# Row maxima of attention scores: turned from columns to rows by VectorE's block transposes instead of TensorE and ScalarE

## The reference

```
x = x + (softmax(Q K^T / 4) V) Wo^T + bo     # Q from layernorm(x), K and V from the context,
                                             # 16 heads of 16 features
h = layernorm(x)
w = softmax(h G) cut to its two largest of 8 experts
out = x + sum_e w_e * down_e(silu(gate_e h) * (up_e h)) + sum_e w_e * loraB_e(loraA_e h)
```

## Time and profile before

| what | value |
|---|---|
| median of 3 runs | 115.64 us (114.97 to 116.44) |
| profiled execution, its own time | 115.25 us |
| its span, first to last instruction | 113.5 us |
| granted TensorE clock, mean | 1.000 of full speed |
| busy TensorE, VectorE | 104.7 us (92%), 89.8 us (79%) |
| busy ScalarE, GpSimd | 70.8 us (62%), 61.5 us (54%) |

### The profile page before, as it was taken

How to read it: one execution, slowest core, us unless ns; L and a number is a source line. 1 busy time by engine, 2 the same in 40 slices (tenths; PEclk the granted TensorE clock), 3 DMA queues, 4 the chain that set the end, 5 groups by cost and what they waited for, 6 DMA issues and landing times.

```text
span 113.5 us, 2548 instructions
## 1 busy us (share of the span) xinstructions
PE 104.7 (92%) x868; PEld 79.6 (70%) x868; DVE 89.8 (79%) x185; ACT 70.8 (62%) x127; POOL 61.5 (54%) x91
## 2 busy tenths in 40 slices
PE   4976999997999999999999999979998899999990
PEld 4656868775776766758676696858565889888680
DVE  5454199998989899799999996968599765589941
ACT  0414562389899869878888899897963504335110
POOL 2268910499859803990588746482729981442000
PEclk9999999999999999999999999999999999999999
DMA  2994788762498003910000400000000000110034
GB/s 60 283 365 190 258 306 249 271 213 78 69 396 326 12 6 129 378 58 0 3 0 6 141 0 6 1 1 0 6 0 0 0 0 0 49 52 3 0 133 147
DMA packets 9405, 11.91 MB, mean 105 GB/s; under 512 B 1008, under 2 KB 6448, under 8 KB 9392
## 3 DMA queue, kind: packets, MB, share of 16 engines
q1 hardware_dynamic: 8672, 11.22, 28.3%
q10 hardware_dynamic: 720, 0.53, 1.5%
HBM read 4.34 MB, written 1.05 MB: 47 GB/s over the span
## 4 chain that ended last, share of the span: by engine, by line
PE 66%; DVE 10%; DMA 7%; POOL 5%; issue 5%; ACT 3%; SPq 1%; POOLq 0%; DVEq 0%
PE unit L766 18%; PE unit L872 12%; PE unit L840 9%; PE unit L773 8%; PE unit L859 7%; DMA wa<-wattn 4%; DMA qstack<-q_lo 3%; POOL attnT L491 3%; PE unit L913 2%; PE unit L911 2%; PE unit L912 2%; DVE rowmax L695 2%; POOL attnT_lo L492 2%; PE unit L846 1%; PE unit L799 1%
## 5 line engine op out<-in xcount | busy, mean ns | idle before, releaser
L695 DVE TENSOR_REDUCE rowmax<-unit 128x4 f32<-128x1024 f32 x32 | 37.5, 1212 | 1.7 <-PE unit L840 1.5
L604 ACT ACTIVATE probs<-unit 128x1024 f32<-128x1024 f32 x32 | 32.2, 1030 | 4.7 <-PE unit L859 4.4
L872 PE MATMUL unit<-probs,vaug 128*32 128x256 f32 x256 | 15.9, 383 | 0.0
L840 PE MATMUL unit<-kstack,qstack 63*128 63x256 f32 x128 | 14.1, 311 | 0.8 <-DVE rowmax L695 0.4
L840 PEld LDWEIGHTS unit<-kstack,qstack 63*128 63x128 f32 x128 | 9.6, 185 | 5.9 <-issue 3.0
L859 PE MATMUL unit<-qstack,kstack 64*128 64x256 f32 x128 | 13.3, 300 | 0.2
L491 POOL TENSOR_SCALAR attnT<-attnT,bias_sb 128x256 f32<-128x256 f32 x8 | 7.7, 957 | 8.6 <-ACT attnT_hi L541 8.2
L859 PEld LDWEIGHTS unit<-qstack,kstack 64*128 64x128 f32 x128 | 9.6, 185 | 3.6 <-issue 1.5
L627 ACT COPY hlT<-unit 128x384 f32<-128x384 f32 x8 | 3.7, 479 | 12.7 <-PE unit L906 12.7
L872 PEld LDWEIGHTS unit<-probs,vaug 128*32 128x32 f32 x256 | 7.3, 109 | 5.1
L459 POOL TENSOR_SCALAR vare<-mv 128x2 f32<-128x2 f32 x8 | 1.8, 223 | 13.2 <-DVE mv L645 12.9
(11 more groups left out here) (97 smaller groups left out, 227.1 us busy)
## 6 DMA issues: line engine op xcount, KB each, us to landing
kstack<-k_hi SPq DMA_DIRECT2D x8, 256.0 KB, 2.7
qstack<-q_hi SPq DMA_DIRECT2D x6, 256.0 KB, 2.8
xs<-x SPq DMA_DIRECT2D x4, 256.0 KB, 3.4
kstack<-k_lo SPq DMA_DIRECT2D x4, 256.0 KB, 2.7
out<-xs SPq DMA_DIRECT2D x8, 128.0 KB, 1.8
cT<-ctxT SPq DMA_DIRECT2D x3, 256.0 KB, 3.7
qstack<-q_lo SPq DMA_DIRECT2D x3, 256.0 KB, 2.9
wf<-wffn SPq DMA_DIRECT2D x1, 648.0 KB, 4.3
```

The source lines that it names most:

```text
L604: act.activation(probs[:, n % NPAIR], unit[PAIR[name, n] // 2][:], ACT.Exp, scale=SCALE).then_inc(exp_done, 1)
L695: dve.tensor_reduce(rowmax[:, b % 2, :, i // 4, :, i % 4].rearrange("p t j -> p j t"), unit[PAIR[name, n] // 2][:], AX.X, ALU.max)\
L840: ins = pe.matmul(dst[:, j, t], qs[rows, PLACE[i], t * P:(t + 1) * P], ks[rows, PLACE[i]], start=True, stop=True)
L872: ins = pe.matmul(dst[QUAD * j:QUAD * (j + 1), i], vaug[:, of % 3, t, 4 * g + j], probs[:, n % NPAIR, j % 2, t], start=(t == 0), stop=(t = ...
```

## The change

The maxima of a half are no longer transposed by TensorE and copied by ScalarE. VectorE does both: four block transposes, one for each 32 partitions of `rowmax`, write `mT` in SBUF. Each reads 32 partitions x 64 elements (two 32x32 blocks, for the two groups of 128 tokens) and writes 32 partitions x 64 elements that always start at partition 0. For that `rowmax` gets 32 columns for each half and group of tokens, of which 8 hold maxima and 24 are zeroed once by GpSimd, and `mT` gets 32 rows, of which the DMA still reads the first 8.

The eight `mrow` stages leave the lists of TensorE and ScalarE and come into VectorE's, each directly behind the fourth or eighth `max` of its batch. All other stages keep their order, but for `ones` (GpSimd's memsets), which goes from behind `minus:2` to the front of its list. PSUM banks that held an `mrow` result go to the next stage of the list without it.

```diff
 "vector":
-    ... max:0.0-3 ln1:2 q:1 max:0.4-7 max:1.0 ln1:3 max:1.1-7
-    u:0 max:2.0-3 u:1 max:2.4-7 u:2 max:3.0 o:0 max:3.1-2 ln2:0 max:3.3 u:3 max:3.4-5 u:4 max:3.6 o:1
-    ln2:1 max:3.7 u:5 route1:0 ...
+    ... max:0.0-3 mrow:0.0 ln1:2 q:1 max:0.4-7 mrow:0.1 max:1.0
+    ln1:3 max:1.1-3 mrow:1.0 max:1.4-7 mrow:1.1 u:0 max:2.0-3 mrow:2.0 u:1 max:2.4-7 mrow:2.1 u:2 max:3.0
+    o:0 max:3.1-2 ln2:0 max:3.3 mrow:3.0 u:3 max:3.4-5 u:4 max:3.6 o:1 ln2:1 max:3.7 mrow:3.1 u:5 ...
 "gpsimd":
-    ln1:0 zero:0 ln1:1 minus:1 zero:1 consts ln1:2 wolo minus:2 ones zero:2 ln1:3 ...
+    ones ln1:0 zero:0 ln1:1 minus:1 zero:1 consts ln1:2 wolo minus:2 zero:2 ln1:3 ...
 "tensor", "scalar":
-    mrow:0.0 mrow:0.1 mrow:1.0 ... mrow:3.1      (each at its place in the list)
...
-        rowmax = sb("rowmax", [P, 2, ST, 2, 2, PAIRS // 2])
-        mT = sb("mT", [PAIRS, 2, S], F32R)
+        rowmax = sb("rowmax", [P, 2, 2, ST, QUAD], F32R)
+        mT = sb("mT", [QUAD, 2, ST, P], F32R)
...
             if name == "mstack":
-                wait_freed(engine, "mrow", 2 * b + i)
+                engine.wait_ge(max_rows, 2 * b + i + 1)
                 engine.dma_start(qstack[b % NSTACK][ROWS:P:HALF]...[:, :, i],
-                                 mT[:, i].bitcast(F32)).then_inc(m_stacked[b % NSTACK][i], 16)
+                                 mT[0:PAIRS, i].bitcast(F32).rearrange("c t p -> c (t p)")).then_inc(...)
...
                 if name == "ones":
+                    pool.memset(rowmax[:, :, :, :, PAIRS:QUAD].bitcast(F32), 0.0).then_inc(row_pads, 1)
+                    pool.wait_ge(row_pads, 1)
...
-                if name == "mrow":                                        # ScalarE
-                    bank, turn = WORK[name, 2 * b + i]
-                    wait_made(act, name, 2 * b + i)
-                    if b:
-                        act.wait_ge(m_stacked[(b - 1) % NSTACK][i], 16 * ((b - 1) // NSTACK + 1))
-                    act.copy(mT[:, i], work[bank][0:PAIRS, 0]).then_inc(work_free[bank], 1)
...
+                if name == "mrow":                                        # VectorE
+                    if b:
+                        dve.wait_ge(m_stacked[(b - 1) % NSTACK][i], 16 * ((b - 1) // NSTACK + 1))
+                    dve.wait_ge(max_done, PAIRS * b + 4 * i + 4)
+                    dve.wait_ge(row_pads, 1)
+                    for n in range(P // QUAD):
+                        tokens = slice(n * QUAD, (n + 1) * QUAD)
+                        ins = dve.transpose(mT[:, i, :, tokens].bitcast(F32), rowmax[tokens, b % 2, i].bitcast(F32))
+                    ins.then_inc(max_rows, 1)
...
-                if name == "mrow":                                        # TensorE
-                    pe.wait_ge(max_done, PAIRS * b + 4 * i + 4)
-                    for t in range(ST):
-                        ins = pe.transpose(dst[0:PAIRS, 0, t * P:(t + 1) * P],
-                                           rowmax[:, b % 2, t, i].rearrange("p j c -> p (j c)"), ident[:])
-                    ins.then_inc(work_ready[bank], 1)
```

More of the change, by code:

```diff
@@ L43 @@
         k:0@0 xT:0@1 qh:0@1 qh:1@0 k:1@2 v:0@1 max:0.0@4 max:0.1@6 xT:1@2 max:0.2@0 max:0.3@4 q:1@2 v:1@3
[L44 to L56, removed]
+        max:0.4@4 max:0.5@6 max:0.6@0 k:2@2 max:0.7@4 attn:0.0@6 xT:2@3 attn:0.1@0 max:1.0@6 attn:0.2@4
+        attn:0.3@0 max:1.1@6 max:1.2@4 q:2@3 max:1.3@0 max:1.4@6 attn:0.4@4 k:3@2 max:1.5@0 xT:3@3 max:1.6@4
@@ new lines @@
+        attn:0.5@6 max:1.7@0 u:0.0@3 u:0.1@3 attn:0.6@4 max:2.0@0 attn:0.7@6 q:3@3 max:2.1@4 attn:1.0@6
+        max:2.2@0 u:1.0@2 max:2.3@4 attn:1.1@6 u:1.1@2 attn:1.2@0 attn:1.3@4 max:2.4@6 v:2@3 max:2.5@0
+        attn:1.4@4 max:2.6@6 u:2.0@2 max:2.7@0 attn:1.5@4 u:2.1@2 attn:1.6@6 attn:1.7@4 max:3.0@0 o:0@2
+        max:3.1@6 attn:2.0@4 u:3.0@3 max:3.2@0 attn:2.1@4 u:3.1@3 max:3.3@6 attn:2.2@0 attn:2.3@4 v:3@2
+        attn:2.4@6 max:3.4@4 max:3.5@2 u:4.0@1 u:4.1@1 attn:2.5@4 attn:2.6@6 max:3.6@2 x2T:0@0 o:1@1 low:0@0
@@ L57 @@
+        attn:2.7@2 max:3.7@4 attn:3.0@6 u:5.0@0 u:5.1@0 attn:3.1@2 attn:3.2@4 attn:3.3@6 glu0:0@0 x2T:1@1
+        glu1:0@2 o:2@3 attn:3.4@0 attn:3.5@4 low:1@2 attn:3.6@6 attn:3.7@0 u:6.0@3 u:6.1@3 u:7.0@2 u:7.1@2
+        x2T:2@3 glu0:1@0 hl:0@1 glu1:1@2 hl:1@3 low:2@4 o:3@0 down:0@1 glu1:2@0 hl:2@2 down:1@3 x2T:3@2
+        down:2@4 glu0:2@5 hl:3@2 low:3@4 glu1:3@1 glu0:3@2 hl:4@0 down:3@4 hl:5@0 down:4@5 hl:6@0 down:5@2
+        hl:7@0 down:6@1 down:7@0
     """,
     "scalar": """
-        biases c:0 cb k:0 xT:0 qh:0 qhih:0 qh:1 k:1 norm1:1 v:0 xT:1 q:1 mrow:0.0 wohi norm1:2 v:1 attn:0.0
@@ L60 @@
[L60 to L64, removed]
@@ L66 @@
+        x2T:1 glu1:0 attn:3.3-6 low:1 attn:3.7 norm2:2 ahi:6 x2T:2 exps:1 glu0:1 ahi:7 hl:1 hl:0 glu1:1 low:2
+        hl:2 exps:2 x2T:3 hl:3 glu0:2 glu1:2 low:3 exps:3 hl:4 glu0:3 glu1:3 hl:5 hl:6 hl:7
     """,
     "vector": """
-        minus:0 ln1:0 norm1:0 ln1:1 k:0 qh:0 k:1 qh:1 max:0.0-3 ln1:2 q:1 max:0.4-7 max:1.0 ln1:3 max:1.1-7
-        u:0 max:2.0-3 u:1 max:2.4-7 u:2 max:3.0 o:0 max:3.1-2 ln2:0 max:3.3 u:3 max:3.4-5 u:4 max:3.6 o:1
-        ln2:1 max:3.7 u:5 route1:0 route2:0 glu0:0 glu1:0 o:2 ln2:2 route3:0 route1:1 u:6 u:7 route2:1 glu0:1
@@ L71 @@
-        route3:1 glu1:1 o:3 ln2:3 route1:2 norm2:3 route2:2 down:2 route3:2 down:0 glu0:2 glu1:2 route1:3
-        route2:3 route3:3 glu0:3 weigh:6 glu1:3 weigh:7 down:4 down:3 down:5 down:6 down:1 down:7
+        minus:0 ln1:0 norm1:0 ln1:1 k:0 qh:0 k:1 qh:1 max:0.0-3 mrow:0.0 ln1:2 q:1 max:0.4-7 mrow:0.1 max:1.0
+        ln1:3 max:1.1-3 mrow:1.0 max:1.4-7 mrow:1.1 u:0 max:2.0-3 mrow:2.0 u:1 max:2.4-7 mrow:2.1 u:2 max:3.0
+        o:0 max:3.1-2 ln2:0 max:3.3 mrow:3.0 u:3 max:3.4-5 u:4 max:3.6 o:1 ln2:1 max:3.7 mrow:3.1 u:5
@@ L73 @@
+        route1:0 route2:0 glu0:0 glu1:0 o:2 ln2:2 route3:0 route1:1 u:6 u:7 route2:1 glu0:1 route3:1 glu1:1
+        o:3 ln2:3 route1:2 norm2:3 route2:2 down:2 route3:2 down:0 glu0:2 glu1:2 route1:3 route2:3 route3:3
+        glu0:3 weigh:6 glu1:3 weigh:7 down:4 down:3 down:5 down:6 down:1 down:7
     """,
     "gpsimd": """
-        ln1:0 zero:0 ln1:1 minus:1 zero:1 consts ln1:2 wolo minus:2 ones zero:2 ln1:3 k:2 q:2 xo:0 xo:1 k:3
+        ones ln1:0 zero:0 ln1:1 minus:1 zero:1 consts ln1:2 wolo minus:2 zero:2 ln1:3 k:2 q:2 xo:0 xo:1 k:3
@@ L202, in xattn_moe_kernel @@
         qzero = [sem(f"qzero{i}") for i in range(NSTACK)]
-        vones = sem("vones")
+        vones, row_pads = sem("vones"), sem("row_pads")
         wf_hi_ready, wf_parts = sem("wf_hi_ready"), sem("wf_parts")
@@ L694, in _ @@
                     dve.wait_ge(s_ready, n + 1)
-                    dve.tensor_reduce(rowmax[:, b % 2, :, i // 4, :, i % 4].rearrange("p t j -> p j t"), unit[PAIR[name, n] // 2][:],
+                    of_pair = rowmax[:, b % 2, i // 4, :, 0:PAIRS].rearrange("p t (j c) -> p j t c", c=4)[:, :, :, i % 4]
+                    dve.tensor_reduce(of_pair, unit[PAIR[name, n] // 2][:],
                                       AX.X, ALU.max)\
                         .then_inc(max_done, 1)
+                if name == "mrow":
[7 more added lines that the diff above has]
+                    ins.then_inc(max_rows, 1)
                 if name == "u":
@@ L779, in _ @@
             for name, b, i, at in plan("tensor"):
-                me = (name, 2 * b + i if name == "mrow" else b)
-                if me in WORK:
-                    bank, turn = WORK[me]
+                if (name, b) in WORK:
+                    bank, turn = WORK[name, b]
                     dst = work[bank]
                     if not (name == "u" and i):
-                        wait_banks(pe, me)
+                        wait_banks(pe, (name, b))
                 if name in ("xT", "x2T"):
```

10 lines of the change are left out of this document (6 added, 4 removed).

## The result

The changed kernel takes 122.56 us (median of 4 runs, 121.4 to 123.57) where the kernel before takes 115.31 us in the same comparison: the ratio is 1.0567, with a 95% interval of 1.0509 to 1.0625. By it the kernel is slower by 6.5 us; 5.5 us had been forecast.

A forecast was written before the change was run, and what follows sets the result against it. VectorE was taken as the bound once its reserve was used: eight stages of 1.03 us less 2.72 us of waits give 5.5 us, and 115.25 + 5.5 = 120.75, forecast as 120.7 us; range 117.7 to 122.4 us.

The forecast's parts named there:

- The bound: While the maxima are made, 15.3 to 69.6 us, VectorE is busy 51.60 of 54.30 us and has almost no room.
- 2.72 us of waits: VectorE's whole reserve up to `u:5`: four waits of 1.82 us together and a fifth of 0.90 us before `u:5`.
- The price of a transpose: One 32x64 transpose on VectorE: 0.25 us, extrapolated from 704 ns for 512 elements a partition and 445 ns for 256.
- full duration without overlap: The four transposes of an `mrow` stage run one after the other on VectorE: 4 x 0.25 = 1.00 us.
- L645's pairs: Two VectorE instructions without a wait take 0.25 us where 2 x 0.166 = 0.33, so the second costs 0.08 us less.
- The overlap case: Rival: a stage's transposes overlap on VectorE, 0.79 us a stage, 3.6 us slower, 118.9 us; chance 0.27.
- The stage: One `mrow` stage on VectorE, lost overlap and gap included: 0.09 + 0.03 + 1.00 - 0.09 = 1.03 us.
- the forecast put at nothing: VectorE's new waits for the pads and the last batch's `mstack` are for things long past and cost nothing.
- 8c - 2.72: Eight stages of 1.03 us on VectorE less its reserve of 2.72 us: `u:5` comes 5.5 us later.
- its saved time becomes waiting: TensorE falls behind from a delay of 0.94 us on; its 0.25 us saved at each `mrow` become waiting.
- The rival that TensorE stays the bound: VectorE's waits up to `u:5` swallow stages of at most 0.34 us; not slower, 113.6 us; chance 0.07.
- the six chain pieces: Six pieces of TensorE's L846 on the chain of waits, 0.22 to 0.32 us each, 1.6 us in all.

The follow-up runs named there:

- The addition alone: Kernel before with all its TensorE and ScalarE work, plus four block transposes of a spare tile on VectorE at each place of the change: ratio 1.0584.
- four spare matmuls: Changed kernel plus four unneeded matmuls in TensorE's list, one ahead of `attn:0.3` and three ahead of `max:1.1`: median 120.33 us, ratio 1.0467.
- One of four: Changed kernel with one block transpose a stage instead of four, three quarters of the maxima staying zero: ratio 0.9949, median 114.67 us.
- Two of four: Changed kernel with two block transposes a stage instead of four, half of the maxima staying zero: ratio 1.0248, median 117.82 us.
- the removal: Kernel before without transposes of the maxima on any engine, `mT` zeroed once and sent when the half's maxima are done: ratio 0.9935.

## Why the prediction was right

- **The bound.** VectorE as the engine that has no room, against the chain and the busy shares, was right. The addition alone gives the whole loss (60.58 us against 60.48), and all of the 2.72 us of waits of the earlier trace rows went.
- **The price of a transpose.** 0.25 us forecast, 233 ns measured. The extrapolation of two shapes with four and eight times the elements was good to 8%.
- **The choice that weighed most,** full duration without overlap, was right: 0.97 us for four, 4 x 0.233 and a little, against 0.61 when all start on the same partitions. The rule of the Trainium skill, VectorE: DVE Perf Modes, section "Two Vector instructions with no wait between them", is borne out by this pair of kernels. Without the holding, each of the later three costs 0.12 us less, (0.97 - 0.61) / 3, where the forecast put 0.08 by L645's pairs. The overlap case would have been 2.7 us cheaper, not 1.9.
- **The stage.** Forecast 1.03 us, and somewhat too low. Counted as the forecast counts, from 0.09 us before the end of the last reduce to the start of what follows, the eight stages of the first profile are 1.13 once, 1.03 once and 1.09 to 1.10 six times: 8.72 us together, where 8 x 1.03 is 8.24. The 1.13 is the stage before `ln1:2`: the moments start 0.04 us after the last transpose ends (23.93 to 23.97). In the kernel in which all four read the same partitions they start 0.06 us before it ends (19.76 + 0.61 = 20.37, start 20.31), so there too the change of partitions is what costs. The six of 1.09 are those from batch 1 on, in which the transposes start 0.09 us after the reduce and not 0.03:

```profile
33.40 3.52 DVE L689 TENSOR_REDUCE rowmax<-unit 128x4 fp32r<-128x1024 f32 x3
37.01 0.97 DVE L699 STREAM_TRANSPOSE mT<-rowmax 32x64 f32<-32x64 f32 x4
```

  From batch 1 on the code has one more wait there, for the last batch's `mstack`, which the forecast put at nothing. The kernel with the addition alone doesn't have it, and there the gap stays 0.03 or 0.04 us (50.68 + 4.58 = 55.26, start 55.30).
- **The sum.** 8c - 2.72 = 5.5 forecast for the stretch, 5.26, 5.31 and 5.36 measured in the profiles of the changed kernel, of the one with four spare matmuls and of the addition alone, where the clock doesn't fall. 43.0 us behind `u:5` stayed 43.0. That it is met this closely is in part luck, as two misses cancel. The stages cost 0.5 us more. Against that, each of the five waits had also cost the overlap of 0.09 us that an instruction without a wait gets, 0.45 us in all, and VectorE's other work in the stretch became shorter (its maxima 37.17 us instead of 37.52, the transposes of `uT` 3.34 instead of 3.52). By this estimate 8.72 - 2.72 - 0.45 - 0.53, and 0.27 for the new wait with its lost overlap, is 5.3. One of four fits the same line. Two of four does so only once the fall is subtracted, and its one execution at a full clock doesn't.
- **What was missing: 1 to 1.6 us.** The forecast said of the stalled TensorE only that its saved time becomes waiting. It took waiting to be free. It isn't: the clock falls in six of eight executions, and in the 3.4 us at half speed TensorE, not VectorE, is the bound. The ratio with the clock kept up, 1.0467, gives 120.7 us from 115.31, the number forecast; the measured 1.0567 times the 115.64 us shown before is 122.2, at the upper end of the range, and this comparison's own median of 122.56 lies just above it; the profiled one of its four executions had the late start. The saved time did "become waiting", L842's waits for `rowmax` growing from 0.4 to 2.7 us; the term that is missing is what the fall behind this waiting costs, 1.5 us in an execution that has it.
- **The rival that TensorE stays the bound** has its point at 0.34 us a stage. With 0.26 us a stage the kernel is indeed not slower (0.9949). But its gain was put too high: the removal is worth 0.7 us (ratio 0.9935) and not the 1.6 of the six chain pieces; that VectorE stands right behind is the likely reason. The Trainium skill, VectorE: DVE Perf Modes, section "Rules for kernel authors", calls VectorE's transpose the fastest for blocks of 32x32. For one instruction that agrees with these traces (233 ns against 273). It doesn't decide this job, which in this form needs four where TensorE needs two, on the engine with no room.

## What to carry to other kernels

Before work goes to an engine, read how long it waited in the stretch where it would get it: that sum is the reserve, and beyond it each added microsecond was a microsecond here. Busy shares of the whole span and the chain of waits don't show it, and a piece taken off the chain is worth only the lead over the engine behind it. Count instructions, not bytes: one transpose over 128 partitions costs about what one over 32 does, and four that start on different partitions stand in a queue. And an engine that begins to wait can cost more than its waits: look at its clock behind them.

## What the runs showed of the hardware

- A block transpose of 64 elements a partition takes 0.23 us over 32 partitions and 0.25 over 128.
- Four that read different groups of 32 partitions take 0.97 us, four that read the same group 0.61.
- TensorE's granted clock fell from full to half for about 3.4 us behind two microseconds in which it was busy 0.70 and 0.29 us, and this cost about 1.5 us: 61.98 and 62.09 us from the first maximum to `u:5` in the two profiles with the fall, 60.53 in the one with about 1 us of spare matmuls in that place. Nine or four of these kept the clock up in eight of eight runs of the changed kernel. With such gaps and no spare matmuls the clock fell in some executions and not in others.
- A spare fp32 matmul of 128x128 by 128 columns, two records in the trace, took 0.26 us in a row of seven (1.83 us).
- Eight matmul records of 128x128 by 256 columns took 1.97 us near the start of one execution and 3.75 us in another, with a granted clock that reads 1.00 in both.
